# Edge counts turned by transposing DMAs instead of TensorE, in a four-layer graph network kernel

## What is computed

```
h = max(layernorm(x), 0);  x = x + L0(h)     # gated graph convolution, 4 rounds
h = max(layernorm(x), 0);  x = x + L1(h)     # h @ W.T, W scattered from edge_weight
h = max(layernorm(x), 0);  x = x + L2(h)     # GCN with self loops
h = max(layernorm(x), 0);  x = x + L3(h)     # graph attention
# L0: deg = segment_sum(1, dst); dis = max(deg, 1) ** -0.5
#     msg = dis[src] * dis[dst] * tanh(u[dst] + v[src]) * x[src]; out += segment_sum(msg, dst)
```

## Time and profile before

| | us |
|---|---|
| median of three runs | 975.7 |
| the three runs | 972.92, 975.7, 976.03 |
| the profiled execution | 974.37 |
| its span, first to last instruction | 972.6 |
| TensorE busy | 955.2 (98%) |
| VectorE busy | 713.5 (73%) |
| ScalarE busy | 496.8 (51%) |

### The profile page before, as it was taken

One profiled execution on the slowest core, in us unless ns is written; L12 is line 12 of the kernel. 1 busy time (PEld: TensorE's weight loads), 2 busy tenths in 40 slices (PEclk: granted clock), 3 DMA queues, 4 the chain that ended last, 5 costly groups with the idle time before them and its releaser, 6 DMA issues.

```text
span 972.6 us, 14172 instructions
## 1 busy us (share of the span) xinstructions
PE 955.2 (98%) x5140; PEld 794.5 (82%) x5140; DVE 713.5 (73%) x1277; ACT 496.8 (51%) x768; POOL 152.0 (16%) x197
## 2 busy tenths in 40 slices
PE   5999999999999999999999999999999999999998
PEld 3888878888888888888888888888888888888887
DVE  7987798788788789558885162797856664967787
ACT  5778864554554557323334344444622323656654
POOL 3022410000000001132223000014210000333331
PEclk9999999999999999999999999999999999999999
DMA  7256491000000005453424400044952220201222
GB/s 258 88 194 230 127 209 68 0 24 0 0 22 0 0 0 119 76 172 131 129 87 126 162 1 1 1 55 116 224 126 77 82 106 0 88 22 66 86 87 82
DMA packets 28472, 83.73 MB, mean 86 GB/s; under 512 B 4696, under 2 KB 4892, under 8 KB 28272
## 3 DMA queue, kind: packets, MB, share of 16 engines
q1 hardware_dynamic: 17536, 53.48, 16.6%
q0 software_dynamic: 10880, 29.50, 12.9%
HBM read 54.65 MB, written 33.57 MB: 91 GB/s over the span
## 4 chain that ended last, share of the span: by engine, by line
PE 95%; DVE 1%; ACT 1%; DMA 1%; issue 1%; POOL 1%; SPq 0%; ACTq 0%; DVEq 0%; POOLq 0%
PE ps L659 22%; PE ps L2492 13%; PE ps L2467 10%; PE ps L2384 9%; PE ps L2386 9%; PE ps L2385 9%; PE ps L2440 5%; PE ps L2436 5%; PE ps L642 3%; PE ps L2307 2%; PE ps L2308 1%; PE ps L2309 1%; PE ps L2232 1%; PE ps L2235 1%; PE ps L2276 1%; PE ps L2503 1%
## 5 line engine op out<-in xcount | busy, mean ns | idle before, releaser
L2384 PE MATMUL ps<-g_hi,mask_hi 128*128 128x512 f32 x400 | 157.7, 394 | 0.2
L2386 PE MATMUL ps<-g_hi,mask_lo 128*128 128x512 f32 x400 | 155.9, 390 | 0.0
L2385 PE MATMUL ps<-g_lo,mask_hi 128*128 128x512 f32 x400 | 155.7, 389 | 0.0
L1232 ACT ACTIVATE mask<-ps,v 128x640 f32<-128x640 f32 x80 | 63.2, 793 | 95.7 <-PE ps L2386 49.1
L2492 PE MATMUL ps<-y_all,att_hi 128*128 128x512 f32 x380 | 103.6, 392 | 0.0
L2384 PEld LDWEIGHTS ps<-g_hi,mask_hi 128*128 128x128 f32 x400 | 75.1, 188 | 19.1 <-DVE mask_lo L1762 2.3
L2386 PEld LDWEIGHTS ps<-g_hi,mask_lo 128*128 128x128 f32 x400 | 75.1, 188 | 16.0
L2385 PEld LDWEIGHTS ps<-g_lo,mask_hi 128*128 128x128 f32 x400 | 75.1, 188 | 14.8
L2467 PE MATMUL ps<-w_hi,parts 128*128 128x512 f32 x280 | 86.7, 389 | 0.0
L659 PE MATMUL ps<-w,hT_hi 128*128 128x512 f32 x320 | 86.6, 392 | 0.0
L625 ACT ACTIVATE hT_hi<-ps 128x1024 fp32r<-128x1024 f32 x30 | 30.8, 1026 | 104.7 <-PE ps L642 104.6
(11 more groups left out here) (248 smaller groups left out, 1989.5 us busy)
## 6 DMA issues: line engine op xcount, KB each, us to landing
xin<-x_after SPq DMA_DIRECT2D x20, 512.0 KB, 3.4
x_after<-g POOLq DMA_DIRECT2D x20, 256.0 KB, 7.6
xres<-x_after POOLq DMA_DIRECT2D x10, 512.0 KB, 3.6
x_after<-xres POOLq DMA_DIRECT2D x10, 512.0 KB, 3.1
xin<-in_x SPq DMA_DIRECT2D x9, 512.0 KB, 3.7
x_after<-in_x SPq DMA_DIRECT2D x8, 512.0 KB
weight_rows<-weight_row POOLq DMA_DIRECT2D x8, 512.0 KB, 3.9
wt_raw<-weight_rows SPq DMA_DIRECT2D x4, 1024.0 KB, 20.5
```

The costliest lines, as they stand in the source:

```text
L1232: nc.scalar.activation(mask[k][:, :], U_ALL, ACT.Tanh, bias=v[:, s:s + 1]).then_inc(tanh_ready, 1)
L2384: nc.tensor.matmul(SUMS[dd], mask_hi[k][:, cols], g_hi[:, s, :], start=(s == 0), stop=False)
L2385: nc.tensor.matmul(SUMS[dd], mask_hi[k][:, cols], g_lo[:, s, :], start=False, stop=False)
L2386: last = nc.tensor.matmul(SUMS[dd], mask_lo[k][:, cols], g_hi[:, s, :], start=False, stop=(s == T - 1))
```

## The change

TensorE's transposes of the counts, their identity matrix in bf16 and VectorE's casts go. SP turns the counts instead: for each tile it issues ten DMAs, each transposing one square of `countT` into a slice of `count_row`, both in SBUF. They wait for the tile's last group and for the DRAM store that last used the buffer. SP does this in its loop over steps three steps late (`TURN_LAG`), behind that step's load and copy; the last tiles follow behind the loop. ScalarE's copy with the row sum now reads and writes `count_row` in place, three places behind instead of two. The weight rows no longer wait for the counts.

```diff
+TURN_LAG = 3
...
+        def turn_counts(a):
+
+            sp.wait_ge(counts_copied, last_group(a) + 1)
+            sp.wait_ge(count_stored[a % 2], 16 * (a // 2))
+            for s in range(T):
+                sp.dma_start_transpose(count_row[a % 2][:, s * P:(s + 1) * P], countT[:, s, a * P:(a + 1) * P]).then_inc(count_transposed[a % 2], 16)
...
             sp.dma_start(x1_dram[(t - 2) * P:(t - 1) * P, :], x[(t - 2) * P:(t - 1) * P, :]).then_inc(rows_stored, 16)
+            for place in range(PER_STEP):
+                for a in tiles_behind(t - TURN_LAG, place, 0):
+                    turn_counts(a)
         sp.dma_start(x1_dram[(T - 2) * P:N, :], x[(T - 2) * P:N, :]).then_inc(rows_stored, 16)
         sp.dma_start(x1_dram[N:NP, :], x[0:NP - N, :]).then_inc(rows_stored, 16)
+        for t in range(T - TURN_LAG, T):
+            for place in range(PER_STEP):
+                for a in tiles_behind(t, place, 0):
+                    turn_counts(a)
...
-        def take_count_rows(a):
-
-            act.wait_ge(count_transposed, a + 1)
-            act.wait_ge(count_stored[a % 2], 16 * (a // 2))
-            nc.scalar.activation(count_row[a % 2][:, :], COUNT_ROWS, ACT.Copy,
+        def sum_count_rows(a):
+
+            act.wait_ge(count_transposed[a % 2], 16 * T * (a // 2 + 1))
+            nc.scalar.activation(count_row[a % 2][:, :], count_row[a % 2][:, :], ACT.Copy,
                                  accum_out=deg[:, a:a + 1]).then_inc(count_row_ready, 1)
...
-            for a in tiles_behind(t, place, 2):
-                take_count_rows(a)
+            for a in tiles_behind(t, place, 3):
+                sum_count_rows(a)
...
-            nc.vector.tensor_copy(count_b[a % 2][:, :, :], countT[:, :, a * P:(a + 1) * P]).then_inc(count_b_ready, 1)
...
-            pe.wait_ge(count_row_ready, a)
+            pe.wait_ge(weights_copied, a)
...
-        def count_rows_pe(a):
-
-            pe.wait_ge(count_b_ready, a + 1)
-            pe.wait_ge(weights_copied, min(a + 1, WT_TILES))
-            pe.wait_ge(count_row_ready, a)
-            for s in range(T):
-                last = nc.tensor.transpose(COUNT_ROWS[:, s * P:(s + 1) * P], count_b[a % 2][:, s, :], ident_b[:, :])
-            last.then_inc(count_transposed, 1)
```

More of the change, by code:

```diff
@@ L242, in build_program @@
     right = [build(f"right{k}", [P, PER_GROUP, CELLS + 3 * WCELLS], BF16) for k in range(RING)]
-    count_b = [build(f"count_b{b}", [P, T, P], BF16) for b in range(2)]
     row_ids = build("row_ids", [P, WINDOWS, 2], BF16)
@@ L247, in build_program @@
     iota_b = build("iota_b", [P, P], BF16)
-    ident_b = build("ident_b", [P, P], BF16)
     b1_all = build("b1_all", [P, HID], F32)
@@ L402, in build_program @@
     weights_taken = sem("weights_taken")
-    count_b_ready = sem("count_b_ready")
-    count_transposed = sem("count_transposed")
+    count_transposed = sems("count_transposed", 2)
     weights_transposed = sem("weights_transposed")
@@ L516, in build_program @@
     ROWS = ps[:, 2 * BANK:4 * BANK]
-    COUNT_ROWS = ps[:, 2 * BANK:2 * BANK + NP // 2].bitcast(BF16)
     FIRST_ROWS = ps[:, 0:WINDOWS]
@@ L923, in _ @@
         nc.gpsimd.memset(countT[:, :, N:NP], 0).then_inc(firsts_done, 1)
-        pool.wait_ge(consts_done, 3)
-        nc.gpsimd.tensor_copy(ident_b[:, :], ident[:, :]).then_inc(consts_done, 1)
         pool.wait_ge(src_landed, 16)
@@ L1526, in _ @@
     def _(dve):
-        dve.wait_ge(consts_done, 5)
+        dve.wait_ge(consts_done, 4)
         d0 = dense[0]
@@ L1622, in place_dve @@
                 cells(n)
-            for a in tiles_behind(t, place, 1):
-                count_rows_of(a)
         def gates(t, count):
@@ L2181, in _ @@
     def _(pe):
-        pe.wait_ge(consts_done, 5)
+        pe.wait_ge(consts_done, 4)
         d0 = dense[0]
@@ L2266, in place_pe @@
                     weight_rows_pe(a)
-            for a in tiles_behind(t, place, 2):
-                count_rows_pe(a)
         def spread_u(q, h):
```

## The result

The changed kernel takes 1048.9 us (median of 4 runs, 1048.16 to 1050.67), the kernel before beside it 975.9 (4 runs, 972.92 to 977.20): the ratio is 1.0755, 95% interval 1.0727 to 1.0784, 73 us slower. The profiled execution took 1049.39, its span is 1047.6 against 972.6, 75.0 us more.

What follows compares the result with a forecast made beforehand. TensorE bounds the kernel at 98% busy, but `deg` decides what follows. SP's start, hundred issues, plain pairs, landing and row sum gave 176.0 against 113.3; 62.7 plus 2 on 974.4 made 1039 us, range 985 to 1085.

Steps and rivals of the forecast that it cites:

- Start: SP's first transposing DMA, for tile 0, can go after the copy of group 2, at 40.6 us.
- x = 1.2 us: Time SP's queue needs from one transposing DMA to the next, taken as 1.2 us, 120 us for a hundred.
- Five pairs, 11.5 us: Five pairs of plain DMAs on SP's queue between the turns, 2.3 us each, midway between issue only and waiting for landing.
- Landing 2.6, row sum 1.3: End of the stage: 2.6 us for the last square to land, then 1.3 us for ScalarE's row sum.
- +2 us for a TensorE that was idle: Behind `deg`, TensorE's product of step 9 and the first masks run slower after idling: 2 us added.
- The waits: ScalarE stalls at tile 0's row sum until 55 us, then at each; TensorE, VectorE and SP's loads of x are delayed.
- SP keeps up for x up to 0.66: SP can turn nine tiles and issue five plain pairs in 63.6 us if each square takes at most 0.66 us.
- One place later costs nothing by itself for tiles 0 to 8: ScalarE's row sum moved one place later was claimed to cost nothing for these tiles.
- rival 2: Faster: squares cost SP nearly nothing or a whole tile queues at once; 5 us less, 969 us; chance 0.04.
- Rival 1: SP's queue keeps up and the stage's end decides: no difference, 974 us, or +3 us; chance 0.09.
- Rival 4: One square at a time on SP's queue, above 1.6 and up to 2.6 us each: up to +203, 1177 us; chance 0.06.
- Rival 5: ScalarE's wait and SP's buffer waits chain up, costing more than SP's own time; given nothing of its own.

## Why the prediction was right, point by point

The forecast was +64.7 us, and the profiled executions differ by 75.0; the verdict, the mechanism and the place were as told, and the time is inside the range. The sum's terms against the trace:

- *Start.* 40.6 forecast, 41.68 measured. The copy of group 2 is 1.1 us later in this profile, ahead of the first turn. The other traces with single squares begin between 40.05 and 41.26, so this is the spread from one execution to the next.
- *x = 1.2 us.* The term that was mis-sized. An undisturbed issue holds the queue 1.234 us, close to the 1.12 and 1.23 of the earlier trace rows on which it rested, but with the gap to the next it is 1.276, and the mean is 1.364, because some issues take up to 2.16: 136.4 instead of 120, +16.4 us, of which 7.6 are the undisturbed pitch and 8.8 the long issues. That the undisturbed issue came so near is in part luck. The rows that gave 1.12 and 1.23 were plain loads of 1 MB and a copy in DRAM, and in the changed kernel plain issues right behind the turns held the queue only 0.50 to 0.62 us, so standing back to back is not what costs 1.2. The Trainium skill's figure for bf16 ("VectorE: DVE Perf Modes", section "The three transpose paths") of 1309 ns a square lies between the undisturbed issue and the mean; its 390 ns for TensorE does not describe this kernel, where ten squares cost 0.56 us.
- *Five pairs, 11.5 us.* They took 6.6 (the gaps between the groups), 1.3 a pair: the squares behind a load don't wait for it to land. 5 us too much, which hid a third of the error in x.
- *Landing 2.6, row sum 1.3.* 1.1 and 1.4. The landing counts from the issue's start, and the sum had already counted the last issue whole: an error of method, 1.5 us.
- *+2 us for a TensorE that was idle.* 1.2 measured. The reason given was a slow pace "though the records grant the full clock"; the one seen here is a granted clock of 0.50.
- *The waits.* ScalarE's ten waits, the first at tile 0 until 56.76 (55 forecast), 13 to 16 us apart, and L2372 at 196.17 (near 185 forecast, with the sum 11 us short) are as told. The load of tile 7 left at 84.08 (near 80 forecast). That casts and transposes removed win nothing behind SP holds too, as far as the terms above give the whole difference without them.
- *SP keeps up for x up to 0.66*, which is 6.6 us a tile. With five squares, 7.2 us a tile, it didn't; with one DMA of 1.42 us a tile it did. No run stands nearer to the limit.
- *"One place later costs nothing by itself for tiles 0 to 8, since nobody waits for a store of counts".* Wrong. Nobody waits for the store, but the weight store and the scales stand behind it on GpSimd. It costs some 3 us, the difference between 975.7 and 973.0 with one square a tile. Behind SP's 75 us it is not seen, and so the verdict did not suffer, but rival 2, at 969 with SP out of the way, was out of this form's reach: one square a tile gave 975.7.
- *Rival 1*, the queue keeps up, did not come. The Trainium skill's rule, transposing DMAs "as fast as regular DMAs" ("Advanced Engine Details and Errata", section "X-Bar Transpose (TRN2)"), does not agree with the trace for single squares, 1.23 us where a plain issue of 512 KB takes 0.34. For ten squares in one it comes near: issued in 1.42 and landed in 4.6, where GpSimd's plain store of the same 320 KB landed in 3.7 in that kernel.
- *Rival 4*, each square landing before the next starts: at the landing of 2.4 us seen here a tile would have needed 24 us; it took 13 to 14.
- *Rival 5*, the stall costs more than SP's own time: excluded for the full kernel, since SP's row has no gap but the pairs. With five squares SP did stand idle once, for 2.3 us.

## What to carry to other kernels

Count the issues of a replacement, not its bytes: a hundred DMAs on one queue are a hundred times the queue's price, here 1.23 to 1.36 us each, and the break-even is (time between two uses) / (issues between them), here an estimate of 0.66 us. If the work is to go by DMA, lay it out so that one issue carries it, give the last piece a buffer that nobody has to empty first (1.7 us here), and try leaving to the engine what stands right before the stage's end, where nothing hides a landing of 4 us. The version that did so was the fastest whole one, 2 us under the kernel before, though its trace doesn't show the reason. When a step is moved a place later, go down every in-order queue that waits for it, the queue of stores too, and ask what stands behind the wait.

## What the runs showed of the hardware

- A transposing DMA's price on the queue hardly depends on its size: 1.229 us for 64 x 128 int16, 1.234 for 128 x 128, 1.42 to 1.58 (medians of three kernels) for ten of these in one. Alone on the queue, one a tile, a 128 x 128 issue took 1.11 us.
- Some of these issues are longer, up to 2.2 us in the full kernel and 3.0 with five squares a tile. Eleven of the fourteen longest began within 6 us after a 512 KB store; with those eight stores at 4 KB the sum of a hundred was 4.1 us less, from one trace on each side, and six long ones remained.
- With TensorE busy for 2.9 of 20 us its mean granted clock was 0.55, with 0.76 of 10 it was 0.50, and ten small matmuls took 2.50 us instead of 1.28; in the next 10 us, busy throughout, the clock averaged 0.87, and then 1.00.
